# Strassen's seven products for the last two feed-forward items of a Macaron block

## The chip, the cores and the metric

The kernel runs on one core of a Trainium2 chip. The metric is the device time of one execution, in microseconds (us). Engines go by the profile's names: PE (TensorE, matmuls), PEld (its weight loads), DVE (VectorE), ACT (ScalarE), POOL (GpSimd), and SP, which issues the transfers.

## The reference

Four sequences of 512 rows and 512 features go through three sublayers, each with a residual:

```python
x = x + 0.5 * ffn(layernorm(x))
x = x + mamba2(layernorm(x))      # the mixer
x = x + 0.5 * ffn(layernorm(x))

def ffn(x):                       # H: Walsh-Hadamard transform, s: sign and scale vectors
    x = H(x * s)
    x = silu(x @ W_gate.T * s) * (x @ W_up.T * s)      # 512 -> 2048
    return H(x * s) @ W_down.T * s                     # 2048 -> 512
```

The transforms are folded into the weights at the start of the kernel. What is left of a feed-forward layer is gate, up and down projections, a silu and a product. All is float32.

## The kernel before

**Precision.** Every large operand is kept as two float32r parts, high and low, and every product is made in three passes (high by high, high by low, low by high; `PASSES`). A high part is a cast by ACT, a low part is the difference to it, mostly by DVE. So 128 hidden features of one sequence cost 4 blocks of the contraction by 3 passes = 12 matmuls of 128x512 (`half_up`).

**Items and chunks.** After the first layer the function `mixer` works through six items. In items 0 to 3 the mixer of one sequence runs beside a feed-forward layer of another; items 4 and 5 are feed-forward alone, the last layer of the last two sequences. A feed-forward item is 8 chunks (`NC`) of 256 hidden features. For a chunk PE runs four groups of 12 matmuls, `gate0`, `up0`, `gate1`, `up1`, and the down projection of the chunk before in four parts of 6 (`down`, one for each 128 rows). Gates go to PSUM bank F[1], ups to F[0], and the parts of `down` alternate between the two. A chunk at large, counted `at` = 8 x item + chunk, runs in this order on PE: `down(at - 1, 0..3)`, `up0(at)`, `gate1(at)`, `up1(at)`, `gate0(at + 1)`.

**Beside PE, for each chunk.** ACT takes the silu of each gate (`silu`), DVE multiplies it by the up (`hidden`), ACT makes the high part (`hidden_high`), DVE the low part (`hidden_low`), and DVE adds each part of `down` to the residual `res` (`add_down`). Each engine executes in the order in which its program is written, and waits on semaphores. POOL has nothing to do in items 4 and 5.

**What is left of the mixer.** The last of the mixer's output projections (`out_proj`, pair 15 of 0 to 15) runs in the second chunk of item 4, with `add_out` on DVE; `sums` (PE), `keep_sums` and `norm` (DVE) give the factor of the normalization, and `ending` (DVE) adds the result to the residual in the third chunk. Then DVE takes the statistics of item 5's rows in three steps (`next(other)`, chunks 3, 4 and 5), ACT normalizes the rows (`beside_row`, after chunk 5), and PE, ACT and DVE transpose and split them in chunk 6 (`beside_turn`) into `fxT`. Item 4's rows stand in `xT`.

**Transfers.** SP loads gate and up weights in pieces of 512 KB into five slots in turn (`load_up`, `up_slot`), each when the piece five before it has been used, and 1 MB of down weights for each chunk into the one tile `wd` (`load_down`).

## Time and profile before

| | |
|---|---|
| three runs | 1640.71, 1641.15, 1642.39 us, median 1641.15 |
| profiled execution, first to last instruction | 1640.3 us |
| around the span (median less span) | about 0.85 us |
| PE busy | 1618.8 us of the span, 99% |
| DVE, ACT, POOL busy | 1039.1, 626.5, 379.5 us |
| items 4 and 5 alone, from the last `down` of item 3 | 1363.4 us to the end |
| transfers, mean | 177 GB/s, 290.5 MB |

The table tells how full each engine is, not what sets the end. That is read from PE's order of work in the stretch that the change touches, and from what each PE group waits for.

### The profile page before, as it was taken

The page shows a single profiled execution, that of the slowest core. Times are in us where ns is not written, and L with a number is a line of the kernel's source. Part 1 is how long each engine was busy: PE and PEld are TensorE (multiplying, and loading weights), DVE is VectorE, ACT ScalarE, POOL GpSimd, SP SyncE. Part 2 cuts the span into 40 slices and gives each one's busy share as a digit, 9 for nine tenths or more (in the row PEclk, how much of TensorE's full clock was granted, in tenths as well). Part 3 has the DMA queues.
Part 4 walks back from the last instruction along what each step waited for, and adds up shares of the span by engine and source line. Part 5 has one row for each costly group of instructions (what it writes and reads, how often), then busy time and mean ns, then how long its engine had stood idle before and what let it go on. Part 6 is the DMA issues. An engine that isn't in the chain of part 4 may idle for free.

```text
span 1640.3 us, 25069 instructions
## 1 busy us (share of the span) xinstructions
PE 1618.8 (99%) x9672; PEld 1310.7 (80%) x9672; DVE 1039.1 (63%) x2045; ACT 626.5 (38%) x934; POOL 379.5 (23%) x298
## 2 busy tenths in 40 slices
PE   7999999999999999999999999999999999999999
PEld 4788888878888778888778888877888878888887
DVE  7543445785677776777776768777775684543333
ACT  5334343464333463333454333355333341122111
POOL 1666662012212212212222122222122121000000
PEclk9999999999999999999999999999999999999999
DMA  7855654755445444454444444445444447556763
GB/s 286 305 200 205 221 193 189 247 183 176 151 156 169 132 166 146 157 168 145 154 164 151 158 161 152 157 143 182 157 159 157 154 130 225 166 183 191 212 204 129
DMA packets 252404, 290.47 MB, mean 177 GB/s; under 512 B 14464, under 2 KB 211200, under 8 KB 243072
## 3 DMA queue, kind: packets, MB, share of 16 engines
q1 hardware_dynamic: 252288, 288.88, 53.4%
q8 instruction: 78, 1.28, 0.3%
q14 instruction: 38, 0.31, 0.1%
HBM read 238.51 MB, written 50.33 MB: 176 GB/s over the span
## 4 chain that ended last, share of the span: by engine, by line
PE 74%; DVE 3%; ACT 1%; issue 1%; DMA 0%; SPq 0%; ACTq 0%; DVEq 0%
PE bank L1189 31%; PE bank L1230 14%; PE bank L1145 12%; PE bank L1258 5%; PE bank L1327 3%; PE bank L1298 2%; PE bank L1314 2%; PE bank L1276 2%; PE bank L1286 1%; PE bank L1321 1%; DVE xT L1748 0%; DVE res L1774 0%; DVE m_cv L1790 0%; DVE m_L L1821 0%; DMA cum_stay<-m_aS 0%
## 5 line engine op out<-in xcount | busy, mean ns | idle before, releaser
L1189 PE MATMUL bank<-fxT,wj 128*128 128x512 f32 x1752 | 415.2, 390 | 0.0
L1189 PEld LDWEIGHTS bank<-fxT,wj 128*128 128x128 f32 x1752 | 328.6, 188 | 68.5
L1230 PE MATMUL bank<-m_wd,m_hb 128*128 128x512 f32 x1128 | 278.8, 393 | 0.0
L1230 PEld LDWEIGHTS bank<-m_wd,m_hb 128*128 128x128 f32 x1128 | 209.2, 188 | 44.9 <-issue 2.5
L1542 ACT CAST m_hb<-xn 128x512 fp32r<-128x512 f32 x96 | 59.5, 620 | 452.6 <-DVE xn L1761 452.6
L1145 PE MATMUL bank<-xT,wi 128*128 128x512 f32 x900 | 222.8, 395 | 1.6 <-DVE m_cv L1790 0.5
L1145 PEld LDWEIGHTS bank<-xT,wi 128*128 128x128 f32 x900 | 166.0, 188 | 39.7 <-issue 5.1
L1774 DVE TENSOR_TENSOR res<-bank,res 128x512 f32<-128x512 f32 x192 | 132.5, 690 | 83.0 <-PE bank L1230 80.9
L2097 POOL TENSOR_TENSOR m_L<-m_L,m_GT 128x512 f32<-128x512 f32 x36 | 52.8, 1466 | 432.8 <-ACT m_L L1551 432.8
L1761 DVE SCALAR_TENSOR_TENSOR xn<-bank,sc,xn 128x512 f32<-128x512 f32 x96 | 71.7, 747 | 121.6 <-PE bank L1189 121.5
L1536 ACT ACTIVATE xn<-bank,sc 128x512 f32<-128x512 f32 x96 | 66.1, 689 | 146.3 <-PE bank L1189 140.8
L1551 ACT ACTIVATE m_L<-bank 128x512 f32<-128x512 f32 x128 | 76.6, 599 | 84.6 <-PE bank L1276 84.3
L1767 DVE TENSOR_TENSOR m_hb<-xn,m_hb 128x512 fp32r<-128x512 f32 x96 | 66.3, 691 | 53.5 <-ACT m_hb L1542 53.5
L511 PE MATMUL bank<-xT,b_wu 128*128 128x512 f32 x384 | 95.7, 397 | 0.0
L1790 DVE SCALAR_TENSOR_TENSOR m_cv<-bank,pr,m_cv 128x511 f32<-128x511 f32 (+2 forms) x117 | 87.3, 746 | 10.5 <-ACT m_cv L1496 7.7
L511 PE MATMUL bank<-b_xT,b_wu 128*128 128x512 f32 x384 | 93.0, 392 | 0.0
L2124 POOL TENSOR_TENSOR m_ss<-m_ss,m_y 128x512 f32<-128x512 f32 x28 | 36.3, 1295 | 239.5 <-ACT m_y L1571 239.5
L1258 PE MATMUL bank<-m_wo,m_yh 128*128 128x512 f32 x384 | 90.7, 391 | 0.7 <-ACT xn L1536 0.7
L552 PE MATMUL bank<-b_wd,b_hb 128*128 128x512 f32 x384 | 91.0, 392 | 0.0
L511 PEld LDWEIGHTS bank<-xT,b_wu 128*128 128x128 f32 x384 | 71.9, 188 | 17.8 <-issue 0.7
L1258 PEld LDWEIGHTS bank<-m_wo,m_yh 128*128 128x128 f32 x384 | 71.6, 188 | 17.7 <-issue 1.9
L511 PEld LDWEIGHTS bank<-b_xT,b_wu 128*128 128x128 f32 x384 | 72.1, 188 | 16.2 <-issue 0.7
(225 smaller groups left out, 2321.3 us busy)
## 6 DMA issues: line engine op xcount, KB each, us to landing
wj<-ug_split SPq DMA_DIRECT2D x167, 512.0 KB, 4.2
m_wd<-dn_split SPq DMA_DIRECT2D x48, 1024.0 KB, 4.9
wi<-in_split SPq DMA_DIRECT2D x76, 512.0 KB, 3.3
ug_split<-b_wu SPq DMA_DIRECT2D x8, 2048.0 KB, 14.1
m_wo<-out_split SPq DMA_DIRECT2D x32, 512.0 KB, 4.1
wi<-ug_split SPq DMA_DIRECT2D x25, 512.0 KB, 4.1
in_split<-b_msp SPq DMA_DIRECT2D x20, 512.0 KB, 3.9
raw<-in_wug SPq DMA_DIRECT2D x8, 1024.0 KB, 6.9
```

The costliest lines, as they stand in the source:

```text
L511: ins = pe.matmul(U[j][:], wu[c % 2][:, a, k, ck(j)], xT[g][:, b, k, :], start=(k == 0 and i == 0), stop=(k == KH - 1 and i == 2))
L552: ins = pe.matmul(down_bank(n, t)[:], hb[:, n % 2, a, j, ck(t)], wd[c % 2][:, b, j, :], start=(j == 0 and i == 0), stop=(j == 1 and i == 2))
L1145: ins = pe.matmul(to[:], w[:, a, k, :], xT[:, b, k, :], start=(k == 0 and i == 0), stop=(k == KH - 1 and i == 2))
L1189: ins = pe.matmul(to[:], w[:, a, k, :], frm[:, b, k, :], start=(k == 0 and i == 0), stop=(k == KH - 1 and i == 2))
L1230: ins = pe.matmul(F[t % 2][:], hb[:, a, j, ck(t)], wd[:, b, j, :], start=(j == 0 and n == 0), stop=(j == 1 and n == 2))
L1258: ins = pe.matmul(F[1 - t % 2][:], yh[:, (2 * pair + i) % 4, a, ck(t)], wout[i][:, b, :], start=(i == 0 and n == 0), stop=(i == 1 and n == 2))
L1536: act.activation(hf[:, j, :], F[1][:], ACT.Silu, scale=sc[:, at % NC, j:j + 1]).then_inc(s_sil, 1)
L1551: act.activation(L[:, b % 2, j, :], A[:], ACT.Exp).then_inc(s_L, 1)
L1761: dve.scalar_tensor_tensor(hf[:, j, :], F[0][:], sc[:, at % NC, 2 + j:3 + j], hf[:, j, :], ALU.mult, ALU.mult).then_inc(s_h, 1)
L1767: dve.tensor_tensor(hb[:, 1, j, :], hf[:, j, :], hb[:, 0, j, :].bitcast(F32), ALU.subtract).then_inc(s_lo, 1)
L1774: dve.tensor_tensor(r, frm[:], r, ALU.add).then_inc(s_acc, 1)
L1790: ins = dve.scalar_tensor_tensor(to[:, d:SEQ], frm[:, 0:SEQ - d], pr[:, w + 3 - d:w + 4 - d], to[:, d:SEQ], ALU.mult, ALU.add)
```

## The change

Items 4 and 5 no longer run one after the other throughout. The new order is: chunks 0 to 2 of item 4 as before (`SOLO` = 3), then chunks 3 to 7 of both items together (`PAIRED` = 5), then chunks 0 to 2 of item 5. `place_of` and `downs` translate the counters.

**The paired chunks.** A unit is 128 hidden features of a chunk, for both sequences; there are ten (`UNITS`). Take gate and up weights as one matrix of 2 x 2 blocks, with the two halves of the contraction (A11, A12 for the gate, A22 and A21 for the up), and both sequences as the other (columns `xT` and `fxT`). The plain product is 8 block products; Strassen's method, in the form of Winograd, makes 7. Each is 2 blocks of the contraction by 3 passes = 6 matmuls. It needs sums of the operands, `s1` to `s4` of the weights for each unit, `t1` to `t4` of the rows once. Products that belong to several results are snapshots: ACT copies a PSUM bank to SBUF between two accumulations. The parts of the down projection (`paired_down`) are spread between the products.

**Who makes the sums.** POOL adds high and low parts of gate and up weights (`gu`) and forms the four sums (`sf`) in `sums_of_weights`; ACT makes the high parts of all four in one instruction of 1024 columns, DVE the low parts. For the rows POOL adds the parts of `xT` (`bf`, 2048 columns), DVE forms t1 and t2 from the PSUM banks of the transposes (`row_differences`), POOL t3 and t4 (`tf`, 1024 columns each), ACT the high parts, DVE (t1, t2) and POOL (t3, t4) the low parts.

**What moves.** Item 5's rows must be in `fxT` before the first unit. So `sums`, `out_proj`, `add_out` and `norm` come in the first chunk of item 4, `ending` too, statistics in the first and second, `beside_row` at the end of the second chunk on ACT and `beside_turn` at the start of the third on PE. `up0` now follows `out_proj` where `gate0` did. A second tile of down weights (`wd2`) and a second hidden tile (`hb1`) are put where `y` and `yh` stood, in turn with the POOL tiles.

PE's program, with POOL's and ACT's beside it (the elementwise functions of DVE are cut):

```diff
-            for at in range(NC * BATCH, NC * ITEMS):
-                down(at - 1, 0, ...); down(at - 1, 1)
-                if q == BATCH and b == 1:
-                    sums(q - 1)
-                down(at - 1, 2); down(at - 1, 3)
-                up0(at)
-                gate1(at)
-                if q == BATCH and b == 6:
-                    for t in range(TPG):
-                        beside_turn(q + 1, t)
-                up1(at)
-                if pair >= 0:
-                    out_proj(pair, at)
-                if at < NC * ITEMS - 1:
-                    gate0(at + 1, pair + 1)
-            down_last(NC * ITEMS - 1)
+            for at in range(MIXED, MIXED + SOLO):          # 32, 33, 34
+                if at == MIXED + SOLO - 1:
+                    for t in range(TPG):
+                        beside_turn(ITEMS - 1, t)
+                for t in range(TPG):
+                    down(at - 1, t, NPAIR * BATCH - 1 if at == MIXED else 0)
+                if at == MIXED:
+                    sums(BATCH - 1)
+                    out_proj(NPAIR * BATCH - 1, at)
+                up0(at, NPAIR * BATCH if at == MIXED else 0)
+                gate1(at)
+                up1(at)
+                if at < MIXED + SOLO - 1:
+                    gate0(at + 1, 0)
+            for u in range(UNITS):
+                unit(u)
+            first = MIXED + SOLO
+            pe.wait_ge(s_acc, pair_downs(PAIRED - 1))
+            half_up(4 * place_of(first), F[1]).then_inc(s_g, 1)
+            half_up(4 * place_of(first) + 1, F[0]).then_inc(s_u, 1)
+            pe.wait_ge(s_cc, 3 * UNITS)
+            for g in range(2):
+                for t in range(TPG):
+                    paired_down(PAIRED - 1, g, t, ending_bank(t))
...
+            def unit(u):
...
+                product(x_bank, a11, b11, True)            # 1
...
+                product(y_bank, a12, b21, True)            # 2
+                pe.wait_ge(s_sl, u + 1)
+                pe.wait_ge(s_tv, TPG + 2)
+                pe.wait_ge(s_sn, 4 * u + 1)
+                product(x_bank, s2, t2, False)             # 3
+                part(0)
+                pe.wait_ge(s_cc, 3 * u + 1)
+                product(y_bank, s1, t1, True)              # 4
+                part(1)
+                pe.wait_ge(s_tp, 4)
+                pe.wait_ge(s_sn, 4 * u + 2)
+                product(x_bank, s3, t3, False)             # 5
+                part(2)
+                pe.wait_ge(s_fxlo, before_item(ITEMS - 1) + TPG)
+                pe.wait_ge(s_sn, 4 * u + 3)
+                product(y_bank, s4, b22, False)            # 6
+                part(3)
...
+                product(x_bank, a22, t4, False)            # 7
...
+            for u in range(UNITS):                         # ACT
+                if u:
+                    paired_high(u - 1, 0)
+                snapshot(u, 0, 1, x_bank)
+                if u:
+                    paired_high(u - 1, 1)
+                else:
+                    sums_of_rows_high(2)
+                snapshot(u, 1, 3, x_bank)
+                paired_silu(u, 0)
+                if u == 0:
+                    sums_of_rows_high(3)
+                if u < UNITS - 1:
+                    sums_of_weights_high(u + 1)
+                snapshot(u, 3, 4, y_bank)
+                snapshot(u, 2, 5, x_bank)
+                paired_silu(u, 1)
...
+            def sums_of_weights(u):                        # POOL
...
+                pool.wait_ge(g_loaded, g_count)
+                wait(pool, s_sl, u)
+                own.done(pool.tensor_tensor(gu[:, 0], wg[:, 0].bitcast(F32), wg[:, 1].bitcast(F32), ALU.add))
+                pool.wait_ge(u_loaded, u_count)
+                own.step(pool.tensor_tensor(gu[:, 1], wu[:, 0].bitcast(F32), wu[:, 1].bitcast(F32), ALU.add))
...
+                own.done(pool.tensor_tensor(sf[:, 2], g1, u1, ALU.subtract))
+                own.step(pool.tensor_tensor(sf[:, 0], u1, u2, ALU.add))
+                own.step(pool.tensor_tensor(sf[:, 1], sf[:, 0], g1, ALU.subtract))
+                pool.tensor_tensor(sf[:, 3], g2, sf[:, 1], ALU.subtract).then_inc(s_sf, 1)
...
+            pool.wait_ge(s_op, TPG * NPAIR * BATCH)
+            pool.wait_ge(s_xlo, TPG * BATCH)
+            pool.tensor_tensor(bf[:], xT[:, 0].bitcast(F32), xT[:, 1].bitcast(F32), ALU.add).then_inc(s_tp, 1)
+            sums_of_weights(0)
+            pool.wait_ge(s_tp, 1)
+            pool.wait_ge(s_tv, TPG)
+            pool.tensor_tensor(tf[:, 2], tf[:, 1], bf[:, 0:2], ALU.subtract).then_inc(s_tp, 1)
+            pool.tensor_tensor(tf[:, 3], bf[:, 2:4], tf[:, 1], ALU.subtract).then_inc(s_tp, 1)
+            for i in (2, 3):
+                pool.wait_ge(s_th, i + 1)
+                pool.tensor_tensor(tb[:, 1, i], tf[:, i], tb[:, 0, i].bitcast(F32), ALU.subtract).then_inc(s_tp, 1)
+            for u in range(1, UNITS):
+                sums_of_weights(u)
```

On DVE, in the third solo chunk: `beside_turn` x4, `add_down` x4, `row_differences(0)` and `(1)`, `hidden(34, 0)`, `hidden_low(34, 0)`, `row_differences(2)` and `(3)`, `sums_of_weights_low(0)`, `hidden(34, 1)`, `hidden_low(34, 1)`, `sums_of_rows_low(0)` and `(1)`; on ACT at its end `silu(34, 1)`, `sums_of_weights_high(0)`, `hidden_high(34, 1)`, `sums_of_rows_high(0)` and `(1)`. In a unit DVE runs `paired_low(u - 1, 0)`, `first_gate(u)`, `paired_low(u - 1, 1)`, then the four adds of the down parts with `sums_of_weights_low(u + 1)`, `second_up` and `second_gate` between them, and `paired_hidden(u, 0)` and `(u, 1)`.

## Rows read from the trace of the kernel before

**Rows 1.** The page: engine totals, and PE's granted clock in 40 slices.
```profile
PE 1618.8 (99%) x9672; PEld 1310.7 (80%) x9672; DVE 1039.1 (63%) x2045; ACT 626.5 (38%) x934; POOL 379.5 (23%) x298
...
PEclk9999999999999999999999999999999999999999
```
**Rows 2.** PE's timeline of items 4 and 5: start, duration, count.
```profile
1363.37 5.61 PE L1230 MATMUL bank<-m_wd,m_hb 128*128 128x512 f32 x24
...
1394.41 5.61 PE L1258 MATMUL bank<-m_wo,m_yh 128*128 128x512 f32 x24
...
1479.26 1.91 PE L1173 MATMUL bank<-cs,m_L 128*128 128x128 f32 x16
1480.92 2.98 PE L1189 MATMUL bank<-xT,wj 128*128 128x512 f32 x12
...
1502.88 5.64 PE L1230 MATMUL bank<-m_wd,m_hb 128*128 128x512 f32 x24
...
1617.70 5.71 PE L1230 MATMUL bank<-m_wd,m_hb 128*128 128x512 f32 x24
...
1631.45 5.61 PE L1241 MATMUL bank<-m_wd,m_hb 128*128 128x512 f32 x24
```
**Rows 3.** DVE's timeline of item 4.
```profile
1391.29 0.16 DVE L129 TENSOR_SCALAR m_rr<-m_rr 128x4 f32<-128x4 f32 x1
...
1394.27 0.16 DVE L139 SCALAR_TENSOR_TENSOR m_rr<-m_rr 128x4 f32<-128x4 f32 x1
...
1400.06 0.69 DVE L1780 TENSOR_TENSOR m_acc<-bank,m_acc 128x512 f32<-128x512 f32 x1 [0.67 <-PE bank L1258]
...
1413.16 2.73 DVE L1920 SCALAR_TENSOR_TENSOR res<-m_acc,m_rr,res 128x512 f32<-128x512 f32 x4
...
1429.56 2.47 DVE L146 BATCH_NORM_STATS2 m_st<-res 128x6 f32<-128x512 f32 x4
...
1449.39 0.75 DVE L1761 SCALAR_TENSOR_TENSOR xn<-bank,sc,xn 128x512 f32<-128x512 f32 x1 [0.66 <-PE bank L1189]
1450.83 0.69 DVE L1767 TENSOR_TENSOR m_hb<-xn,m_hb 128x512 fp32r<-128x512 f32 x1 [0.69 <-ACT m_hb L1542]
```
**Rows 4.** ACT's timeline of item 4.
```profile
1450.17 0.62 ACT L1542 CAST m_hb<-xn 128x512 fp32r<-128x512 f32 x1 [2.92 <-DVE xn L1761]
...
1469.05 2.92 ACT L1613 ACTIVATE m_L<-res,m_mv 128x512 f32<-128x512 f32 x4
```
**Rows 5.** POOL's groups by form: line, count | busy, mean ns | idle before.
```profile
L2118 POOL TENSOR_TENSOR m_yh<-m_y,m_yh 128x512 fp32r<-128x512 f32 x32 | 41.2, 1288 | 12.2 <-ACT m_yh L1563 12.2
...
L413 POOL TENSOR_TENSOR b_t<-raw 128x1024 f32<-128x1024 f32 x14 | 33.6, 2418 | 44.9 <-DMA raw<-in_wug 26.8 <-DVE last L713 17.9
```
**Rows 6.** DVE's groups by form.
```profile
L785 DVE TENSOR_TENSOR b_t<-raw 128x1024 f32<-128x1024 f32 x2 | 2.4, 1222 | 1.7 <-DMA raw<-in_wug 1.7
```
**Rows 7.** ACT's groups by form.
```profile
L1633 ACT ACTIVATE m_dc<-bank 128x384 f32<-128x384 f32 x4 | 1.9, 486 | 9.1 <-PE bank L1352 9.1
```
**Rows 8.** POOL's and DVE's timeline, where both run.
```profile
1328.84 1.30 POOL L2114 TENSOR_TENSOR m_y<-m_y,m_zs 128x512 f32<-128x512 f32 x1
1329.01 1.15 DVE L137 TENSOR_TENSOR m_mv<-m_mv 128x4 f32<-128x4 f32 x1
```
**Rows 9.** DVE's timeline beside it: an instruction of 512 columns, and the next.
```profile
1339.27 1.28 DVE L1821 TENSOR_TENSOR m_L<-m_L,m_GT 128x512 f32<-128x512 f32 x1
1340.47 0.68 DVE L1748 TENSOR_TENSOR xT<-bank,xT 128x512 fp32r<-128x512 f32 x1
```
**Rows 10.** POOL's and PE's timeline of the same stretch.
```profile
1338.71 1.29 POOL L2097 TENSOR_TENSOR m_L<-m_L,m_GT 128x512 f32<-128x512 f32 x1 [8.34 <-ACT m_L L1551]
...
1341.30 0.63 PE L1155 MATMUL bank<-cs,xn 128*128 128x128 f32 x4 [0.24 <-DVE xT L1748]
```
**Rows 11.** PE's first instructions: counts, then durations in ns, least, median and most.
```profile
L467 PE MATMUL bank<-res,b_H x4: 1061/1061/1191, 8.6 to 11.3; 128*128 128x512 f32 x4
...
L467 PE MATMUL bank<-res,b_H x16: 592/592/1191, 8.6 to 20.9; 128*128 128x512 f32 x16
```

More of the change, by code:

```diff
@@ L1062, in _ @@
             load_in(6)
-            for q in range(ITEMS):
-                mix, more, other = q < BATCH, q < BATCH - 1, q < ITEMS - 1
+            for q in range(BATCH):
+                more = q < BATCH - 1
                 m0 = NIN * q + 3
@@ new lines, in solo_down @@
+            def solo_down(t):
+                at = MIXED + SOLO - 1
+                if t == 0:
+                    pe.wait_ge(s_wd, 16 * (at + 1))
+                    pe.wait_ge(s_hi, 2 * at + 2)
+                    pe.wait_ge(s_lo, 2 * at + 2)
+                    pe.wait_ge(s_tv, TPG)
+                elif t == 2:
+                    pe.wait_ge(s_h, 2 * at + 2)
+                    pe.wait_ge(s_sil, 2 * at + 2)
+                for j in range(2):
+                    for n, (a, b) in enumerate(PASSES):
+                        ins = pe.matmul(banks[4 + t][:], hb[:, a, j, ck(t)], wd[:, b, j, :], start=(j == 0 and n == 0), stop=(j == 1 and n == 2))
+                ins.then_inc(s_d, 1)
@@ L1723, in _ @@
+            first = MIXED + SOLO
+            paired_high(UNITS - 1, 0)
+            paired_high(UNITS - 1, 1)
+            silu(first, 0)
+            for at in range(first, LAST):
+                hidden_high(at, 0)
                 silu(at, 1)
                 hidden_high(at, 1)
-                if at < NC * ITEMS - 1:
+                if at < LAST - 1:
                     silu(at + 1, 0)
-                if q == BATCH and b == 5:
-                    for t in range(TPG):
-                        beside_row(q + 1, t)
@@ L1730, in _ @@
-                if q == BATCH and b == 6:
-                    for t in range(TPG):
-                        beside_turn(q + 1, t)
         @block.vector
@@ new lines, in _ @@
+            for t in range(TPG):
+                add_down(at - 1, t)
+            for t in range(TPG):
+                add_out(NPAIR * BATCH - 1, t)
+            keep_sums(BATCH - 1)
+            norm(BATCH - 1)
+            hidden(at, 0)
+            hidden_low(at, 0)
+            ending(BATCH - 1)
+            hidden(at, 1)
+            hidden_low(at, 1)
+            dve.wait_ge(s_fin, TPG * BATCH)
+            next(other)
+            at = MIXED + 1
+            for t in range(TPG):
+                add_down(at - 1, t)
@@ new lines, in _ @@
+            next(other)
+            hidden(at, 0)
+            hidden_low(at, 0)
+            next(other)
+            bias(1, s_fs)
+            hidden(at, 1)
+            hidden_low(at, 1)
+            at = MIXED + 2
+            for t in range(TPG):
+                beside_turn(ITEMS - 1, t)
+            for t in range(TPG):
+                add_down(at - 1, t)
+            row_differences(0)
+            row_differences(1)
+            hidden(at, 0)
+            hidden_low(at, 0)
+            row_differences(2)
@@ new lines, in _, with part @@
+            row_differences(3)
+            sums_of_weights_low(0)
+            hidden(at, 1)
+            hidden_low(at, 1)
+            sums_of_rows_low(0)
+            sums_of_rows_low(1)
+            for u in range(UNITS):
+                p, j = u // 2, u % 2
+                def part(t):
+                    if p:
+                        add_paired(p - 1, j, t, banks[4 + t])
+                    elif j == 0:
+                        add_solo(t)
+                if u:
+                    paired_low(u - 1, 0)
+                first_gate(u)
+                if u:
+                    paired_low(u - 1, 1)
+                part(0)
+                if u < UNITS - 1:
+                    sums_of_weights_low(u + 1)
+                part(1)
+                second_up(u)
+                part(2)
+                second_gate(u)
+                part(3)
+                paired_hidden(u, 0)
+                paired_hidden(u, 1)
@@ new lines, in _ @@
+            first = MIXED + SOLO
+            paired_low(UNITS - 1, 0)
+            paired_low(UNITS - 1, 1)
+            hidden(first, 0)
+            for g in range(2):
+                for t in range(TPG):
+                    add_paired(PAIRED - 1, g, t, ending_bank(t))
+            hidden_low(first, 0)
+            hidden(first, 1)
+            hidden_low(first, 1)
+            for at in range(first + 1, LAST):
+                for t in range(TPG):
+                    add_down(at - 1, t)
```

349 lines of the change are left out of this document (270 added, 79 removed).

## The prediction

> **What bounds the kernel now.** I read the page first: PE is busy for 99% of the span at a granted clock of 1.00 in every slice [rows 1]. Busy is not yet bound, so next comes PE's timeline of items 4 and 5. There one group follows another without a gap, from 1363.37 to the last group at 1631.45 [rows 2]. From the `down` at 1502.88 to that at 1617.70 are 7 chunks of 72 matmuls: 114.82 / 504 = 0.228 us for a matmul of 128x512, 1.37 us for a group of 6, 2.73 for one of 12. So in this stretch each matmul taken away is worth 0.228 us, as long as nothing takes its place. Then I read DVE's, ACT's and POOL's timelines for durations and hand-overs, because the change puts a web of waits where PE had none.
>
> **What it takes away.** A unit has 7 products of 6 matmuls in place of 8. 10 units x 6 = 60 matmuls, 60 x 0.228 = 13.7 us. Down groups, transposes, `sums` and `out_proj` stay in number. Nothing of this lies beside other work: it is the whole gain.
>
> **What it adds.** PE's new work is only waits, so the sum is a walk along PE's new program. Hand-overs: after PE's last matmul of a group DVE begins 0.2 to 0.3 us later than the next group would start, ACT 0.2; from ACT to DVE and back 0.03; from DVE to PE 0.15 (1340.47 + 0.68 to 1341.30 [rows 9, 10]). Durations: an add of a bank 0.69, `hidden` 0.75, a low part 0.69 [rows 3], a high part 0.62 [rows 4]; a row of several such instructions runs at 0.61 each on DVE (2.73 for four of 0.69, some overlap) and 0.53 on ACT. Of 1024 columns: DVE 1.22 [rows 6], POOL 2.42 [rows 5]. Not shown: ACT at 1024 columns, between 0.62 and twice that; from 0.486 at 384 [rows 7] to 0.62 at 512 the slope is about 1 ns a column, I take 1.05. POOL at 2048 and 256 columns: its slope is (2.418 - 1.288) / 512 = 2.2 ns [rows 5], so 4.7 and 0.73, between bounds of 2.4 to 4.8 (once to twice 1024) and 0 to 1.29.
>
> **Exclusion of DVE and POOL.** One more price decides the sum. At 1328.84 POOL starts 1.30 us of work; DVE's instruction on 4 columns at 1329.01, which costs 0.16 elsewhere, takes 1.15 and ends with POOL's [rows 3, 8]. An instruction of 512 columns started at 1339.27 under POOL's of 1338.71 to 1340.00 ends 0.55 after POOL's end [rows 9, 10]: it got nothing done before. Both have their inputs in SBUF. I take it that a DVE instruction with both inputs in SBUF waits out a POOL instruction, and goes next when POOL's ends; those that read a bank do not. The Trainium skill says this too (SBUF — State Buffer, Who interferes with whom): DVE with two SBUF inputs and POOL's reads exclude each other for whole instructions. By that rule the sum is the one below; without it, it is the first rival.
>
> The walk, in the order of PE's program (s: stall):
>
> 1. **Chunk 32.** `down` ends at 1368.8, `sums` 0.8 later; `out_proj` waits for the last add of `down` in bank F[1], done 1369.7: s 0.2. It ends at 1375.3. `up0` now needs the bank of `out_proj`'s last part; before, `gate0` stood between, and the add ran beside it (1400.06, [rows 3], while `out_proj` had ended by 1394.41 + 24 x 0.228 = 1399.9 [rows 2]). Add done at 1376.2: s 1.0.
> 2. POOL starts `bf` when `out_proj` has ended: 4.7 us, 1375.5 to 1380.2. `norm` (1391.29 to 1394.43, 3.1 us of tiny instructions [rows 3]) starts at 1376.4 and is shut out until then: about 12 of its 16 steps, 2.4 us, follow. `hidden(32, 0)` starts at 1382.6, `up1` needs it at 1381.8 and gets it at 1383.4: s 1.6. Without exclusion this is nothing.
> 3. `ending` (2.73 [rows 3]) stands before `hidden(32, 1)`: low part done at 1389.4, `gate0` over at 1388.9: s 0.6. The statistics (2.47) stand before the first `add_down` of chunk 33: `down` part 2 waits 0.3.
> 4. **`beside_turn`.** On ACT the four `beside_row` (2.92 us [rows 4]) stand behind `silu(34, 0)`, which needs `gate0(34)`, and on PE the transposes come directly after `gate0(34)`. Let that be time 0. Silu to 0.9, rows to 3.7, last transposes to 4.3. The same 16 cost 1480.92 - 1479.26 = 1.7 before [rows 2]: s 2.6. The four low parts (`fxT`) stand before `add_down(33, ..)`: s 0.5.
> 5. **Before product 3 of unit 0.** `up1(34)` ends at 18.4, products 1 and 2 at 21.2. Product 3 needs the low part of t2. DVE ends `row_differences` at 17.1; POOL then takes tf2 to 19.5. `sums_of_weights_low(0)` could start at 17.6, is shut out to 19.5 and ends at 20.6; POOL's tf3, 20.6 to 23.1. `hidden(34, 1)` to 21.4, its high part to 22.0, its low part shut out to 23.1, ends 23.7. Then t1's and t2's low parts, 1.2 each: 25.9, PE at 26.0: s 4.8 (2.4 without exclusion).
> 6. **Before product 6 of unit 0.** This is a chain of four engines in program order. Product 3 ends at 27.4. ACT: snapshot to 28.2, silu 28.8, high part of t4 29.8. POOL: its low part, 2.42, to 32.3; only then `sums_of_weights(1)`: 2 x 1.29 + 4 x 0.73 + 5 waits on itself of some 0.06 = 5.7, to 38.0. ACT: `sums_of_weights_high(1)`, for the next unit but ahead of the snapshot that product 6 needs: 39.0; snapshot 39.6, PE 39.7. PE has between 27.4 and then only 5 groups of 6, to 34.2: s 5.5.
> 7. **Unit 1** has no down parts; product 6 waits for the snapshot behind the weights' high part: s 0.3. **Units 2 to 9** have 66 matmuls, 15.0 us. Their tightest wait is the snapshot of product 1's bank, at 2.2 us after the unit's start and needed at 2.7. DVE has about 9.5 us of work there, ACT 6, POOL 5.7, and a POOL instruction of at most 1.3 us in DVE's way fits the slack elsewhere. I take 0.2 for unit 2, where POOL runs late, and 0 for the rest. After unit 9 the eight down parts use four banks and DVE adds one in 0.69 for 1.37 of PE: 0.
>
> Transfers: the paired chunks use 3 MB in about 30 us where 16.4 had to do, and each load waits for a group at least a unit before its use; 0. The new `wd2` load is behind t3 only, and needed two units later.
>
> Sum of stalls: 0.2 + 1.0 + 1.6 + 0.6 + 0.3 + 2.6 + 0.5 + 4.8 + 5.5 + 0.3 + 0.2 = 17.6. Net 17.6 - 13.7 = +3.9 on a profiled execution of 1640.3, 1644.2; the median stands 0.85 above that span, so 1645.1.
>
> **The rivals.** (a) *No exclusion on these operands*, or much less: then steps 2, 3 and 5 lose 1.6, 0.6 and 2.4, stalls 13.0, net -0.7: 1640.5, not slower. For: only a few cases stand in the trace, all with short operands. Against: they all say the same. It decides from 4 us of stall less on. For a time more than 0.2% faster POOL's chain in step 6 would have to be 3 us shorter too, which its two instructions of 512 columns and four of 256 don't allow unless small ones cost nearly nothing (the lower bound, 4 x 0.73 = 2.9).
>
> (b) *PE's clock falls after the long stalls.* In the trace the clock is granted at 1.00 throughout [rows 1], and PE never pauses for long after the start. But its first four matmuls, after 8.6 us without work, take 1061 ns where the same instruction takes 592 later [rows 11]: 0.47 us more each, 1.9 for the four, one level down (1.2 in place of 2.4 GHz). If a pause of 4.8 or 5.5 us does the same, 1.9 each: 1647.0 with one, 1648.9 with both. The Trainium skill (TensorE: Matmul & The Clock Gate, HAM oscillation) says that pauses of a few microseconds between bursts bring the half clock back. No pause of that size in this trace shows it.
>
> (c) *POOL gets in again before the waiting DVE instruction* in step 5: tf3 follows tf2, t2 is 1.6 later; with POOL's steps slowed by DVE in step 6 up to 1 more: 1647.7.
>
> (d) *A wait in each unit*: 0.4 us in eight units is 3.2: 1648.3. Its place would be product 3 behind the snapshot.
>
> **How the numbers follow.** What three runs of this kernel can tell from no change is about 0.2%, 3.3 us. Forecast 1645.1: chance 0.38, own range 1643 to 1647. (a) 0.22, (b) 0.25, (c) 0.08, (d) 0.07. Slower by over 0.2% is above 1644.4: 0.25 of the forecast's 0.38, all of (b), (c), (d) but a little: 0.63. Same: 0.13 of the forecast, 0.15 of (a), 0.01 of the others: 0.29. Faster: 0.07 of (a), with other terms short as well, and a remainder: 0.08. The range reaches from (a)'s near side, 1641, to (b) with both falls and some of step 6's upper bounds, 1650.5.
>
> **What would show it.** PE's timeline: two pauses, of about 5 us before the third and sixth product of unit 0, one ended by DVE's low part, one by ACT's snapshot; the transposes stretched to 4.3 us; units of 15.0 us with no pause; PE's matmuls fewer by 60 and its span of items 4 and 5 longer by some 4 us. DVE's 512- and 1024-column instructions on SBUF operands longer than 0.69 and 1.22 under POOL's. Wrong would be: POOL and DVE running at full speed side by side, durations of 0.39 us for PE's matmuls that turn to 0.6 after a pause, or small pauses at each unit's start.

## The result, and the profile after

| | median us (lowest to highest, runs) | span of the profiled execution | mean clock |
|---|---|---|---|
| before | 1641.77 (1640.71 to 1642.45, 4) | 1640.3 | 1.00 |
| after | 1649.98 (1649.54 to 1651.13, 4) | 1648.2 | 0.995 |

The ratio is 1.005 [1.0036, 1.0064]: 8.2 us slower. That is inside the range as a whole (1641 to 1650.5), but outside the forecast's own (1643 to 1647), twice its +3.9, and 1.1 us above what rival (b) gives with both falls of the clock (1648.9). The page after, engine totals:

```profile
PE 1614.2 (98%) x9612; PEld 1304.1 (79%) x9612; DVE 1083.5 (66%) x2095; ACT 660.6 (40%) x988; POOL 454.1 (28%) x363
```

The 60 matmuls are gone, but PE's busy time fell by 4.6 us against [rows 1], not by 13.7. Up to the tail (items 4 and 5) it is the same in both (1345.1 and 1345.6 us). So part of the loss is in slower matmuls, not in waiting. PE's timeline of items 4 and 5 after, which answers to [rows 2] (start, duration, group, count, and in brackets the idle time before it and what ended it):

```profile
1362.96 5.62 PE L1306 MATMUL bank<-m_wd,m_hb 128*128 128x512 f32 x24
...
1375.97 5.69 PE L1263 MATMUL bank<-xT,wj 128*128 128x512 f32 x24 [0.83 <-issue]
1383.89 7.35 PE L1263 MATMUL bank<-xT,wi 128*128 128x512 f32 x24 [2.23 <-DVE xn L2026]
1391.08 5.70 PE L1306 MATMUL bank<-m_wd,m_hb 128*128 128x512 f32 x24
...
1409.18 2.77 PE L1247 MATMUL bank<-cs,m_qs 128*128 128x128 f32 x16 [1.48 <-ACT m_qs L1845]
1411.70 3.02 PE L1306 MATMUL bank<-m_wd,m_hb 128*128 128x512 f32 x12
1414.88 3.01 PE L1306 MATMUL bank<-m_wd,m_hb 128*128 128x512 f32 x12 [0.15 <-DVE res L2039]
...
1433.26 2.90 PE L1343 MATMUL bank<-m_tb,m_sb 128*128 128x512 f32 x6 [4.45 <-DVE m_tb L2063]
1435.96 2.76 PE L1336 MATMUL bank<-m_wd,m_hb 128*128 128x512 f32 x6
1438.52 1.61 PE L1343 MATMUL bank<-m_tb,m_sb 128*128 128x512 f32 x6
...
1448.15 2.23 PE L1343 MATMUL bank<-fxT,m_sb 128*128 128x512 f32 x6 [3.95 <-ACT m_qs L1740]
1450.18 2.55 PE L1336 MATMUL bank<-m_wd,m_hb 128*128 128x512 f32 x6
...
1463.92 2.90 PE L1343 MATMUL bank<-xT,wj 128*128 128x512 f32 x12
...
1639.34 5.63 PE L1407 MATMUL bank<-m_wd,m_hb 128*128 128x512 f32 x24
```

Read it by starts. From the first of these groups to the last it is 276.4 us, where [rows 2] have 268.1: all of the loss, 8.3 us, is here. Up to the start of unit 2, at 1463.92, it is 100.96 us; I call this stretch the head of the tail, since nearly all that the experiments change lies in it. A pause can be read in two ways, and both are used below: as the bracket has it, with the modelled end of the group before, or as the difference of two starts less 0.228 us for each matmul between them. The three long ones are 2.23, 4.45 and 3.95 us by the brackets and 2.45, 4.6 and 4.1 by starts.

The two pauses forecast before the third and sixth product are there, ended by what was forecast. What the forecast did not have: 24 matmuls in 7.35 us behind the first pause, and groups of 6 in 2.7 where they should take 1.37. Durations of single matmuls, behind the second pause and later (ns, least, median, most; first and last start):

```profile
L1343 PE MATMUL bank<-m_tb,m_sb x6: 628/628/767, 1433.3 to 1435.5; 128*128 128x512 f32 x6
L1343 PE MATMUL bank<-m_tb,m_sb x19: 389/389/395, 1467.8 to 1482.9; 128*128 128x512 f32 x19
```

And the granted clock of such stretches (stretch, length, busy time of PE, PEld, DVE, ACT and POOL, then the clock, DMA share, GB/s):

```profile
1386.00:1388.00 2.00, 2.00 (x7) 1.59 (x6) 1.86 (x3) 0.00 (x0) 0.00 (x0) 0.62 0.00 0
1433.20:1436.00 2.80, 2.74 (x7) 2.19 (x8) 0.56 (x1) 0.00 (x0) 2.18 (x1) 0.50 0.00 0
1436.00:1438.50 2.50, 2.50 (x7) 1.94 (x6) 0.00 (x0) 2.14 (x3) 0.09 (x1) 0.50 0.31 88
1450.20:1452.60 2.40, 2.40 (x8) 1.87 (x7) 1.78 (x3) 0.58 (x1) 2.32 (x3) 0.55 0.00 0
1463.92:1584.68 120.76, 120.76 (x529) 99.00 (x528) 69.95 (x95) 44.84 (x72) 40.32 (x41) 1.00 0.33 105
```

At 0.50, the lower of the two levels (1.2 GHz), PE runs behind the pause of 4.6 us; behind those of 2.45 and 4.1 the stretches read 0.62 and 0.55, so PE ran a part of each at the lower level. From unit 2 on the clock is 1.00 and eight units take 120.76 us, 15.1 each, without a pause. DVE and POOL behind `out_proj`, which answers to [rows 3, 8]:

```profile
1375.97 4.11 DVE L129 TENSOR_SCALAR m_rr<-m_rr 128x4 f32<-128x4 f32 x1
1380.12 0.17 DVE L130 TENSOR_SCALAR m_rr<-m_rr 128x4 int32<-128x4 int32 x1
...
1383.09 0.75 DVE L2026 SCALAR_TENSOR_TENSOR xn<-bank,sc,xn 128x512 f32<-128x512 f32 x1
```
```profile
1375.38 4.68 POOL L2557 TENSOR_TENSOR m_bf<-xT 128x2048 f32<-128x2048 f32 x1 [7.62 <-PE bank L1426]
```

The first of the 16 small steps of `norm` takes 4.11 us where it costs 0.16 in [rows 3], and ends with POOL's `bf` (1380.06). The other fifteen follow, and PE's `up1` waits for all of them.

DVE and POOL ahead of product 3:

```profile
1425.07 3.04 DVE L2068 TENSOR_TENSOR m_sb<-m_sf,m_sb 128x1024 fp32r<-128x1024 f32 x1 [0.59 <-ACT m_sb L1766]
1428.03 0.73 DVE L2026 SCALAR_TENSOR_TENSOR xn<-bank,sc,xn 128x512 f32<-128x512 f32 x1
1429.45 1.43 DVE L2032 TENSOR_TENSOR m_hb<-xn,m_hb 128x512 fp32r<-128x512 f32 x1 [0.68 <-ACT m_hb L1729]
1430.81 2.35 DVE L2063 TENSOR_TENSOR m_tb<-m_tf,m_tb 128x1024 fp32r<-128x1024 f32 x2
```
```profile
1424.62 2.41 POOL L2561 TENSOR_TENSOR m_tf<-m_tf,m_bf 128x1024 f32<-128x1024 f32 x1 [8.28 <-DVE m_tf L2058]
1426.98 3.35 POOL L2562 TENSOR_TENSOR m_tf<-m_bf,m_tf 128x1024 f32<-128x1024 f32 x1
```

DVE's low part of the weight sums takes 3.04 us in place of 1.22, beside POOL's t3; POOL's t4 then takes 3.35 in place of 2.41, beside that low part; and the low part of the last `hidden` takes 1.43 in place of 0.69, beside t4. The `hidden` between them reads a bank, runs while POOL works on t4, and takes its usual 0.73.

### The profile page after: what moved, and what is told of

Its sections match the earlier page's. It is cut to its first block, busy times and chain, and to the rows that moved or that the text cites. A ratio compares the mean times of both kernels' runs of the same rounds, so it can differ in the third digit from the quotient of the medians.

```text
span 1648.2 us, 25144 instructions
## 1 busy us (share of the span) xinstructions
PE 1614.2 (98%) x9612; PEld 1304.1 (79%) x9612; DVE 1083.5 (66%) x2095; ACT 660.6 (40%) x988; POOL 454.1 (28%) x363
## 4 chain that ended last, share of the span: by engine, by line
PE 72%; DVE 3%; ACT 2%; issue 2%; POOL 1%; DMA 0%; SPq 0%; ACTq 0%; DVEq 0%; POOLq 0%
PE bank L1263 24%; PE bank L1219 12%; PE bank L1306 10%; PE bank L1343 5%; PE bank L1426 5%; PE bank L1320 3%; PE bank L1495 3%; PE bank L1466 2%; PE bank L1482 2%; PE bank L1444 2%; PE bank L1454 1%; PE bank L1489 1%; DVE xT L2013 0%; DVE res L2039 0%; PE bank L1247 0%
## 5 line engine op out<-in xcount | busy, mean ns | idle before, releaser
L1263 PE MATMUL bank<-fxT,wj 128*128 128x512 f32 x1608 | 381.5, 390 | 0.0
L1263 PEld LDWEIGHTS bank<-fxT,wj 128*128 128x128 f32 x1608 | 301.6, 188 | 62.8
L1306 PE MATMUL bank<-m_wd,m_hb 128*128 128x512 f32 x864 | 216.8, 393 | 0.2 <-DVE res L2039 0.2
L1729 ACT CAST m_hb<-xn 128x512 fp32r<-128x512 f32 x76 | 47.1, 620 | 353.2 <-DVE xn L2026 345.4
L1306 PEld LDWEIGHTS bank<-m_wd,m_hb 128*128 128x128 f32 x864 | 160.4, 188 | 33.7 <-DVE res L2039 0.8
L2039 DVE TENSOR_TENSOR res<-bank,res 128x512 f32<-128x512 f32 x148 | 102.0, 690 | 33.2 <-PE bank L1306 31.1
L2026 DVE SCALAR_TENSOR_TENSOR xn<-bank,sc,xn 128x512 f32<-128x512 f32 x76 | 56.7, 746 | 67.7 <-PE bank L1263 67.5
L1723 ACT ACTIVATE xn<-bank,sc 128x512 f32<-128x512 f32 x76 | 52.3, 689 | 120.3 <-PE bank L1263 114.7
L2122 DVE SCALAR_TENSOR_TENSOR m_cv<-bank,pr,m_cv 128x511 f32<-128x511 f32 (+2 forms) x117 | 87.3, 746 | 10.5 <-ACT m_cv L1681 7.7
L511 PEld LDWEIGHTS bank<-xT,b_wu 128*128 128x128 f32 x384 | 71.9, 188 | 17.8 <-issue 0.7
L1426 PEld LDWEIGHTS bank<-m_wo,m_yh 128*128 128x128 f32 x384 | 71.5, 188 | 17.8 <-issue 1.9
L552 PEld LDWEIGHTS bank<-b_wd,b_hb 128*128 128x128 f32 x384 | 71.8, 188 | 15.8 <-issue 0.8
```

The costliest lines, as they stand in the source:

```text
L511: ins = pe.matmul(U[j][:], wu[c % 2][:, a, k, ck(j)], xT[g][:, b, k, :], start=(k == 0 and i == 0), stop=(k == KH - 1 and i == 2))
L552: ins = pe.matmul(down_bank(n, t)[:], hb[:, n % 2, a, j, ck(t)], wd[c % 2][:, b, j, :], start=(j == 0 and i == 0), stop=(j == 1 and i == 2))
L1263: ins = pe.matmul(to[:], w[:, a, k, :], frm[:, b, k, :], start=(k == 0 and i == 0), stop=(k == KH - 1 and i == 2))
L1306: ins = pe.matmul(F[t % 2][:], hb[:, a, j, ck(t)], w[:, b, j, :], start=(j == 0 and n == 0), stop=(j == 1 and n == 2))
L1426: ins = pe.matmul(F[1 - t % 2][:], yh[:, (2 * pair + i) % 4, a, ck(t)], wout[i][:, b, :], start=(i == 0 and n == 0), stop=(i == 1 and n == 2))
L2026: dve.scalar_tensor_tensor(hf[:, j, :], F[0][:], sc[:, place_of(at) % NC, 2 + j:3 + j], hf[:, j, :], ALU.mult, ALU.mult).then_inc(s_h, 1)
```

## The experiments

Each kernel is the changed one with the edit shown. The columns: median; the kernel before on the same chip; ratio with interval; and PE's head of the tail in the profiled execution. The kernels e1 to e4 ran on one chip, e5 to e8 on another, e9, e10 and the changed kernel again on a third, so medians are compared through the ratio. The 1360 us ahead of the tail, which no edit touches, took 1361.6 (e5_solo4) to 1367.5 us (e8_tf_late, whose profiled execution was its longest) in these executions, so the head of the tail is the sharper measure of an edit.

| run | median | before | ratio | head of the tail |
|---|---|---|---|---|
| the changed kernel | 1649.98 | 1641.77 | 1.0050 [1.0036, 1.0064] | 100.96 |
| the changed kernel again | 1651.81 | 1643.43 | 1.0049 [1.0037, 1.0062] | 101.88 |
| e1_fill | 1648.47 | 1642.33 | 1.0036 [1.0025, 1.0046] | 97.44 |
| e2_bf_late | 1647.36 | 1642.33 | 1.0028 [1.0019, 1.0038] | 97.65 |
| e3_turn_late | 1650.68 | 1642.33 | 1.0047 [1.0032, 1.0062] | 100.52 |
| e4_act_order | 1648.51 | 1642.33 | 1.0034 [1.0022, 1.0046] | 97.55 |
| e5_solo4 | 1651.15 | 1642.78 | 1.0052 [1.0037, 1.0067] | 116.58 (one chunk of 16.4 more) |
| e6_all3 | 1645.16 | 1642.78 | 1.0013 [1.0002, 1.0023] | 95.19 |
| e7_order | 1640.16 | 1642.78 | 0.9986 [0.9977, 0.9996] | 90.15 |
| e8_tf_late | 1651.20 | 1642.78 | 1.0050 [1.0032, 1.0067] | 101.62 |
| e9_order2 | 1632.11 | 1643.43 | 0.9930 [0.9917, 0.9944] | 81.87 |
| e10_turn_tf | 1647.56 | 1643.43 | 1.0026 [1.0017, 1.0035] | 98.10 |

**The clock alone.** PE's three long pauses are filled with matmuls on data that lie ready, into a bank whose content nobody reads: 9 before `up1(32)`, 18 before product 3 of unit 0, 22 before product 6.

```diff
+            def filler(n):
...
+                for _ in range(n):
+                    pe.matmul(A[:], xT[:, 0, 0, 0:P], xT[:, 0, 1, :], start=True, stop=True)
```

> The changed kernel with matmuls of 128x512 on idle data put into three of PE's pauses, shorter than the pauses: 9 before up1 of chunk 32, 18 before product 3 and 22 before product 6 of unit 0. They write a PSUM bank that nobody reads. Theory (the pauses bring the clock down, and PE's matmuls after each run at half rate): granted clock 1.00 in the whole tail, no matmul of 0.63 us after the pauses, and 4 to 5 us less than the changed kernel (1.7 + 1.4 + 1.7), although PE does 49 matmuls more: about 1645.3. Rival (the groups are slow because their operands were just written, or for want of bandwidth): they stay slow, time as before or up to 2 us more: 1650 to 1652.

PE's timeline of e1_fill:

```profile
1386.08 5.76 PE L1263 MATMUL bank<-xT,wi 128*128 128x512 f32 x24 [0.19 <-DVE xn L2038]
1392.35 5.80 PE L1306 MATMUL bank<-m_wd,m_hb 128*128 128x512 f32 x24 [0.52 <-DVE m_hb L2044]
...
1434.71 1.62 PE L1343 MATMUL bank<-m_tb,m_sb 128*128 128x512 f32 x6 [0.40 <-issue]
...
1442.98 5.19 PE L1351 MATMUL bank<-xT 128*128 128x512 f32 x22
1448.39 1.63 PE L1343 MATMUL bank<-fxT,m_sb 128*128 128x512 f32 x6 [0.22 <-ACT m_qs L1752]
```

Every group runs at full pace, and 49 matmuls more make the kernel shorter: 3.5 us by the head of the tail, 2.3 by the ratios, whose intervals overlap. That is less than the 4.6 that the three falls cost (worked out below), because a wait stands behind the first one: with the slow group (7.35) `hidden(32, 1)` came in time, with the fast one (5.76) PE waits 0.52 for it (0.8 by starts). The granted clock is 1.00 from 1380 to 1470 us. From product 3 to product 6 it is 13.68 us, where the forecast had 13.7 and the changed kernel has 14.89. The pauses and their causes are as forecast, and the clock is what lay on top.

**Exclusion of DVE and POOL.** `bf`, POOL's 4.68 us, goes behind `ending`'s statistics.

```diff
             pool.wait_ge(s_xlo, TPG * BATCH)
+            pool.wait_ge(s_fs, BATCH)
             pool.tensor_tensor(bf[:], xT[:, 0].bitcast(F32), xT[:, 1].bitcast(F32), ALU.add).then_inc(s_tp, 1)
```

> The changed kernel, but POOL's sum of 2048 columns (bf) waits for the statistics of item 5, some 28 us later. Theory (POOL's instruction shuts out norm on DVE, up1 of chunk 32 waits for it, and the clock falls): norm takes 3.1 us from its first to its last step in place of 7.1, the pause of 2.45 us before up1 goes, and with it the slow matmuls behind it (1.7): 3.5 to 4.2 us less, about 1646. Rival (norm is late because of out_proj alone, DVE and POOL do not exclude each other): the 4.1 us of norm's first instruction stay, 1650.

DVE's and POOL's timelines of e2_bf_late:

```profile
1401.87 2.47 DVE L2032 TENSOR_TENSOR m_hb<-xn,m_hb 128x512 fp32r<-128x512 f32 x1 [0.69 <-ACT m_hb L1729]
```
```profile
1399.11 4.68 POOL L2558 TENSOR_TENSOR m_bf<-xT 128x2048 f32<-128x2048 f32 x1 [31.92 <-DVE m_mv L2008]
```

`norm`'s first step took 0.17, and `up1` started 5.54 us after `up0`, without a pause or a slow matmul: 2.4 us of waiting and 1.7 of clock, 4.2 in all, are gone together. In its new place `bf` shuts out a low part of 512 columns (2.47 for 0.69), which here had slack. The net is 3.3 us: the slower matmuls behind product 6 cost 2.5 us in this execution where they cost 1.7. (The pause before product 6 reads 5.05 in place of 3.95 only because the slow matmuls ahead of it were fewer: from product 3 to product 6 it is 14.87 us, as in the changed kernel.) Rival (a) is out at this place: the same steps cost nothing extra without `bf` beside them, and a low part that has it beside it is shut out.

The other place, before product 3: POOL's instructions for t3 and t4 (tf2 and tf3 in the prediction, `tf[:, 2]` and `tf[:, 3]` here) wait until the low parts of t1 and t2 are done on DVE.

```diff
             pool.wait_ge(s_tp, 1)
-            pool.wait_ge(s_tv, TPG)
+            pool.wait_ge(s_tv, TPG + 2)
             pool.tensor_tensor(tf[:, 2], tf[:, 1], bf[:, 0:2], ALU.subtract).then_inc(s_tp, 1)
```

> The changed kernel, but POOL forms t3 and t4 only when DVE has made the low parts of t1 and t2. A test of the exclusion. Theory: the low part of the weight sums takes 1.22 us in place of 3.04, that of the last hidden part 0.69 in place of 1.43, and the pause before product 3 falls from 4.45 to about 2.0 us; POOL's chain starts later, so products 5 and 6 wait longer, and the sum is 0 to 2 us more: 1650 to 1652. Rival (DVE's long instructions come from the operands or the transfers): their durations stay, the pause before product 3 stays, and the later pauses grow: 1653 or more.

PE's timeline of e8_tf_late:

```profile
1435.54 1.63 PE L1343 MATMUL bank<-m_tb,m_sb 128*128 128x512 f32 x6 [2.25 <-DVE m_tb L2063]
...
1442.72 1.66 PE L1343 MATMUL bank<-m_tb,m_sb 128*128 128x512 f32 x6 [1.47 <-POOL m_tb L2565]
...
1452.28 2.90 PE L1343 MATMUL bank<-fxT,m_sb 128*128 128x512 f32 x6 [6.54 <-ACT m_qs L1740]
```

The forecast's "2.4 without exclusion" is there: by starts the pause is 2.39 us in place of 4.6, and DVE's two low parts took 2.36 together. The kernel is no faster, since POOL's chain is now late: 1.47 before product 5, 6.54 before product 6. So the exclusion costs 2.2 us at this pause, and a pause is not worth its size: what fills it is late elsewhere.

**The transposes.** PE's 16 transposes, and DVE's adds of them, go behind the four `down` parts and `add_down` of chunk 33.

```diff
+                for t in range(TPG):
+                    down(at - 1, t, NPAIR * BATCH - 1 if at == MIXED else 0)
                 if at == MIXED + SOLO - 1:
                     for t in range(TPG):
                         beside_turn(ITEMS - 1, t)
-                for t in range(TPG):
-                    down(at - 1, t, NPAIR * BATCH - 1 if at == MIXED else 0)
```

> The changed kernel, but the transposes of item 5's rows come behind the down projection of chunk 33 instead of ahead of it, on PE and on DVE. Theory (PE waits for ACT's row instructions, which a down projection of 5.5 us covers): the 16 transposes take 1.7 us in place of 4.15, and the 0.56 us pause in the down projection goes: 3.0 us less, 1647.0. Rival (a wait moved, not removed: DVE's low parts and row differences come later and push product 3 of unit 0): the pause before product 3 grows by what is won, 1649 to 1650.

PE's, DVE's and POOL's timelines of e3_turn_late:

```profile
1413.19 1.91 PE L1247 MATMUL bank<-cs,m_qs 128*128 128x128 f32 x16
...
1432.98 2.90 PE L1343 MATMUL bank<-m_tb,m_sb 128*128 128x512 f32 x6 [6.97 <-DVE m_tb L2063]
```
```profile
1426.23 6.65 DVE L2063 TENSOR_TENSOR m_tb<-m_tf,m_tb 128x1024 fp32r<-128x1024 f32 x2
```
```profile
1422.28 3.48 POOL L2561 TENSOR_TENSOR m_tf<-m_tf,m_bf 128x1024 f32<-128x1024 f32 x1 [5.84 <-DVE m_tf L2058]
1425.71 2.81 POOL L2562 TENSOR_TENSOR m_tf<-m_bf,m_tf 128x1024 f32<-128x1024 f32 x1
1428.48 3.32 POOL L2565 TENSOR_TENSOR m_tb<-m_tf,m_tb 128x1024 fp32r<-128x1024 f32 x1
```

The 16 transposes take 1.9 us again and wait for nothing, and product 3 waits 2.5 us longer. Its chain now runs inside POOL's three instructions of 1024 columns, and the two engines take turns: DVE's pair takes 6.65 where it took 2.35 in the changed kernel. Nothing is won. With POOL held back as in e8_tf_late the same move pays:

> The changed kernel with the transposes behind the down projection and POOL's t3 and t4 after DVE's low parts. The first alone won nothing, since POOL then shut DVE out for 6.65 us before product 3. Theory (what the transposes win was eaten by the exclusion): without it the pause before product 3 is about 2.3 us, not 7, and the 3 us show: 1647 to 1649, 3 us below the run with the second edit alone. Rival (product 3 is bound by another chain that starts with the transposes): the pause before it stays over 4 us, 1651.

The pause before product 3 is 2.25 as in e8_tf_late, and the start of unit 2 comes 3.5 us earlier than there (98.10 for 101.62; ratio 1.0026 for 1.0050, where the intervals overlap from 1.0032 to 1.0035). The transposes' 3 us of step 4 are real; DVE and POOL shutting each other out swallowed them in e3_turn_late.

**The order on ACT.** The weights' high and low parts for unit 1 go behind unit 0's snapshots and parts; the diff is ACT's, DVE's `sums_of_weights_low` moves likewise, behind `part(3)`.

```diff
                 if u == 0:
                     sums_of_rows_high(3)
-                if u < UNITS - 1:
+                if 0 < u < UNITS - 1:
                     sums_of_weights_high(u + 1)
                 snapshot(u, 3, 4, y_bank)
                 snapshot(u, 2, 5, x_bank)
+                if u == 0:
+                    sums_of_weights_high(u + 1)
                 paired_silu(u, 1)
```

> The changed kernel, but in unit 0 alone ACT makes the high parts of unit 1's weight sums after the two snapshots of unit 0, and DVE their low parts after its last add. Theory (product 6 of unit 0 waits for a snapshot that stands behind POOL's chain in ACT's order, 4.1 us and a fall of the clock worth 1.7): the pause before product 6 goes, but unit 1 needs the same sums before its third product, and gets them and its first snapshot about 2 us late: net 3 to 4 us less, 1646 to 1647. Rival (POOL's chain bounds unit 1 as well, the wait only moves): a pause of 4 us before product 3 of unit 1, 1649 to 1650.

PE's timeline of e4_act_order, unit 1:

```profile
1451.40 1.63 PE L1343 MATMUL bank<-m_tb,m_sb 128*128 128x512 f32 x6 [0.33 <-ACT xn L1740]
1453.84 3.02 PE L1343 MATMUL bank<-m_tb,m_sb 128*128 128x512 f32 x12 [0.81 <-DVE xn L2077]
1458.31 1.63 PE L1343 MATMUL bank<-fxT,m_sb 128*128 128x512 f32 x6 [1.45 <-ACT xn L1740]
```

The pause before product 6 of unit 0 is gone, and its clock fall. Half of it comes back as three waits in unit 1, since POOL's chain is as late as ever: 3.4 us net (2.6 by the ratios). This execution has a fall of its own at another place. Behind the pause of 2.23 us it kept the clock (24 matmuls in 5.75 us), and lost it behind the shorter one before the transposes:

```profile
1408.99 3.23 PE L1247 MATMUL bank<-cs,m_qs 128*128 128x128 f32 x16 [1.48 <-ACT m_qs L1845]
1411.88 6.88 PE L1306 MATMUL bank<-m_wd,m_hb 128*128 128x512 f32 x24
```

The granted clock is 0.50 from 1411.80 to 1414.00, and transposes and `down` take 1.05 us longer than in the changed kernel, where the same pause of 1.48 us had no fall behind it. In one kernel with e2 and e3:

> The three edits together: bf late, transposes behind the down projection, and the sums of unit 1 behind the snapshots. Each alone: minus 3.3, 0 and minus 3.4 us of the tail in the profile. Theory: they add up but for the falls of the clock, and the transposes still win nothing, because POOL shuts DVE out before product 3 (a pause of 7 us there): 6 to 7 us less than the changed kernel, level with the kernel before within 0.15%. Rival (the pauses share a cause that stays): less than 4 us.

The head of the tail is 5.8 us shorter than in the changed kernel. Left are 6.97 before product 3, 1.61 before `down` of chunk 33 (its hidden part, shut out by `bf`) and the three of unit 1.

**Fewer paired chunks.** SOLO is 4 in place of 3: one chunk less in pairs, so two units less.

> The changed kernel with four chunks alone and four in pairs (SOLO = 4) in place of three and five. Theory (the units give what their matmuls say, all loss lies in the opening, whose price does not depend on the number of units): 12 matmuls more, 2.73 us, less some 0.1 for the hand-overs of two units: 1652.6 on the chip where the changed kernel takes 1650, that is 10.8 us above the kernel before. Rival (the units lose about as much as they give): no difference, 8.2 above.

The ratio is 1.0052 for 1.0050: inconclusive. Its profiled execution has no clock fall behind the pause of 2.2 us (24 matmuls in 5.74, then 0.53 of wait), which makes that stretch 0.8 us shorter than in the changed kernel. The tail was 278.25 against 276.38, 1.9 longer; with the 0.8 the chunk is worth 2.7, as the sum of matmuls says. That is one execution of each.

**The new order as a whole.** All that made PE wait is moved: the edits of e2 and e3, and of e4 with the weights behind all of unit 0. POOL keeps only `bf` and the weight sums, DVE makes tf2, tf3 and their low parts inside unit 0, and product 3 waits for t2 alone. The core of it, on ACT and DVE:

```diff
+                if end:
+                    sums_of_rows_high(1)
+                    sums_of_rows_high(0)
                 hidden_high(at, 1)
-                if end:
-                    sums_of_rows_high(0)
-                    sums_of_rows_high(1)
-                else:
+                if not end:
...
+                if u == 0:
+                    dve.wait_ge(s_tv, TPG)
+                    dve.tensor_tensor(tf[:, 2], tf[:, 1], bf[:, 0:2], ALU.subtract).then_inc(s_tp, 1)
+                    dve.tensor_tensor(tf[:, 3], bf[:, 2:4], tf[:, 1], ALU.subtract).then_inc(s_tp, 1)
+                    sums_of_rows_low(2)
                 part(0)
```

> The changed kernel with bf late, the transposes behind the down projection, and the opening of unit 0 in another order: DVE, not POOL, makes t3 and t4 and their low parts (1.2 us each in place of 2.4, no exclusion), t2's low part comes first, ahead of the last hidden parts, product 3 waits for it alone, and unit 1's sums follow when all this is done. PE's matmuls are the same. Theory (all loss is waits at the opening, set by order and by POOL and DVE excluding each other): no pause over 1 us behind the third solo chunk, clock 1.00, 16 to 18 us less than the changed kernel: 1632 to 1634, 0.5% to 0.6% below the kernel before. Rival (DVE's added 4.9 us become the new wait, at product 5 or 7 of unit 0 or product 3 of unit 1): pauses of 3 to 5 us there, 1637 to 1640.

PE's timeline of e7_order:

```profile
1407.00 5.73 PE L1306 MATMUL bank<-m_wd,m_hb 128*128 128x512 f32 x24 [1.58 <-DVE m_hb L2033]
...
1449.68 2.90 PE L1343 MATMUL bank<-fxT,m_sb 128*128 128x512 f32 x6 [3.84 <-ACT xn L1741]
1452.38 2.76 PE L1343 MATMUL bank<-m_tb,wj 128*128 128x512 f32 x6
```

It is faster than the kernel before, by 0.14%, and 6 us above the upper end of what was expected; the rival's 1637 to 1640 is nearer. Unit 0 has no pause but 0.56, and `down` of chunk 33 waits 1.58 for a low part that `bf` shuts out. The wait has moved one unit on: ACT's high part of the weights for unit 2 stands ahead of the snapshots of unit 1 and waits for POOL, and PE waits 3.84 and runs two groups at half clock. The last run takes this order away in unit 1 too (on DVE likewise), and puts `bf` behind the low parts of chunk 33; its edit is shown against e7_order:

```diff
-                if 0 < u < UNITS - 1:
+                if 1 < u < UNITS - 1:
                     sums_of_weights_high(u + 1)
...
-                if u == 0:
-                    sums_of_weights_high(1)
+                if u < 2:
+                    sums_of_weights_high(u + 1)
...
-            pool.wait_ge(s_fs, BATCH)
+            pool.wait_ge(s_lo, 2 * (MIXED + SOLO - 1))
```

> The reordered kernel with two more moves: bf waits for the last low part of chunk 33, which it shut out for 1.8 us; and in unit 1, as in unit 0, the sums of the next unit come after the snapshots, since the pause of 3.84 us before its product 6 was the same wait one unit later. Theory: both pauses (1.6 and 3.8 us) and the fall of the clock behind the second (2.6) go, PE's tail is 8 us shorter than in the reordered kernel: 1631 to 1633 where the kernel before takes 1642, 0.6% faster. Rival (POOL's chain of 5.7 us for each unit's sums needs a unit with down parts to hide, so that unit 2 waits in turn): a pause of 2 to 4 us before product 3 of unit 2, 1635 to 1638.

All that PE waits for between 1362 and 1446 us in e9_order2 (us in total, times, longest), from the view of waits by engine:

```profile
PE bank L1263 <- issue: 0.8, 1, 0.8
PE bank L1343 <- ACT m_qs L1741: 0.6, 1, 0.6
```

The clock is 1.000. The kernel takes 1632.11 us (1630.49 to 1633.08, 5 runs), ratio 0.993 [0.9917, 0.9944]: 11.3 us faster than the kernel before. Its tail is 257.6 us, 10.5 shorter than before; 60 matmuls are 13.7, less 3.2 us of hand-overs: 1.3 in chunk 32 as in the changed kernel, 0.7 before product 3, the rest in steps of 0.3 us and less. So three quarters of what seven products save can be had.

The changed kernel once more, on this chip:

> The changed kernel itself once more, beside the others on this chip. Theory and rival alike: 8 us above the kernel before; with the clock falling behind two or three of the pauses, not always the same ones, so that its runs spread over 3 us or so.

It repeats the result: its five runs lie between 1650.28 and 1654.00, at a mean clock of 0.994 to 0.996, where e9_order2's lie within 2.6 us at 1.000. That the falls make this spread of 3.7 us is not shown: the kernel before spread by 4.8 us on this chip, over 15 runs, at 0.998 to 1.000.

## Why the prediction was right, and where it was short

The numbers of the changed kernel are differences of starts on PE, less 0.228 us for each matmul of 128x512 (and less what `sums` and the transposes cost before).

| step | forecast | measured |
|---|---|---|
| 60 matmuls | -13.7 | -13.7 |
| 1, chunk 32 | 0.2 + 1.0 | 0.2 + 1.05 |
| 2, `norm` behind `bf` | 1.6 | 2.45, and 1.7 of clock |
| 3, behind `ending` | 0.6 + 0.3 | 0.1 |
| 4, `beside_turn` | 2.6 + 0.5 | 2.5 + 0.6 |
| 5, product 3 | 4.8 | 4.6 |
| 6, product 6 | 5.5 | 5.5, and 1.2 of clock before it, 1.7 behind |
| 7, units 1 to 9 | 0.3 + 0.2 | 0.4 + 0.4 |
| sum of stalls | 17.6 | 17.8 without the clock, 22.4 with it |
| net | +3.9 | +8.7 by this sum, +8.3 by the tail, +8.2 by the medians |

The walk was right: the places, what ends each wait, and a sum off by 0.2 us, in which two errors of 0.8 cancel by luck. Three terms failed. That the time lay in the range at all is owed to (b): the forecast's own mechanism ended at 1647, and the upper end was put at 1650.5 for both falls of the clock and some of step 6's upper bounds. One of the signs that the prediction named for being wrong came true with them, matmuls that turn from 0.39 us to 0.6 after a pause (0.389 and 0.628 above), and items 4 and 5 are 8.3 us longer where it had some 4.

**The clock, 4.6 us: the choice between forecast and rival (b).** I had [rows 11] as a bound for a pause of 8.6 us, took "no pause of that size shows it" as a reason to leave the clock at 1.00, and gave (b) 0.25. The rows after show falls behind 2.45, 4.6 and 4.1 us. The matmuls behind them took 1.7, 2.6 and 1.7 us longer than at full clock, where [rows 11] gave 1.9. Of the 2.6 only 1.2 count: they are the delay of product 3, which the chain to product 6 passes on, and the slow part of `down` behind it ran in time that PE would have waited. That makes the 4.6. e1_fill takes the clock alone away. (b) was the mechanism, with three places and not two: the short pause of 2.2 us, which it did not name, costs a fall too, though not in each execution (e4_act_order and e5_solo4 ran the group behind it in 5.75 and 5.74 us). The rule that I cited (the Trainium skill, TensorE: Matmul & The Clock Gate, HAM oscillation) is borne out by the rows in its direction: pauses of a few microseconds between bursts brought the half clock back.

**Step 2, 0.85 us short.** I let four of `norm`'s 16 steps pass before POOL had the port. None passed: `bf` started 0.6 us ahead of the first of them. By my own times, `bf` from 1375.5 and `norm` from 1376.4, none should have. The fifteen steps behind `bf` take 2.97 us where I had 2.4, 0.6 of the 0.85; the rest is spread over the hand-overs around them.

**Step 3, 0.8 us too much in the changed kernel, right in e1_fill.** There, with the clock up, PE's `down` starts 0.8 us late and loses 0.2 more inside, for 0.6 + 0.3 forecast; behind the slow `up1` and `gate0` it hid. A clock fall and a wait behind it share their cost.

The other rivals: (a), no exclusion, fell by e2_bf_late and e8_tf_late. The rule cited for it (the Trainium skill, SBUF — State Buffer, Who interferes with whom) held in the rows: DVE instructions with two inputs in SBUF and POOL's waited each other out whole, and a DVE instruction that reads a bank did not wait (0.73 us beside POOL's t4; in e7_order 0.75 in the midst of `bf`). The forecast put it down to two inputs in SBUF alone, and there it is too narrow: the step that waited 4.11 us for `bf` (line 129, a `tensor_scalar` on 4 columns) has one. No run separates the kinds further. (c), POOL getting in ahead of the waiting DVE instruction: in the changed kernel it did not at product 3, where low part, t4 and low part took turns; e3_turn_late shows the same through POOL's three instructions. (d), a wait in each unit: none, 15.1 us each. The forecast of POOL's chain in step 6 was right because the sizes were (1024 columns 2.40, 256 0.72 to 0.74; in step 2, 2048 columns 4.68), and ACT's 1024 columns took 1.04 for an assumed 1.05.

What stays open: what decides, at a pause of about 1.5 to 2.2 us, whether the clock falls. The profiled executions differ there with the same program ahead of it.
